# Groups' rows in a ViT block with routed experts: loaded as 32x32 blocks and transposed by VectorE

## What is computed

```python
xt = x.reshape(-1, d)                               # 2304 tokens x 192, after layernorm
route_prob = softmax(xt @ Ws + bs, axis=-1)         # 9 experts
p, routes = max(route_prob), argmax(route_prob)
h = gelu(einsum('td,edf->tef', xt, W1) + b1)        # 192 -> 768
out = einsum('tef,efd->ted', h, W2) + b2            # 768 -> 192
common = out[:, 0, :]
sel = out at routes
final = where(routes == 0, common * scaling, pe * sel + (1 - pe) * common)
```

## Time and profile before

| | us |
|---|---|
| median of 3 runs | 387.95 |
| lowest and highest | 387.5, 389.18 |
| the profiled execution | 386.88 |
| its span, first to last instruction | 385.0 |
| TensorE clock granted, mean over the span | 0.993 |

### The profile page before, as it was taken

The page is one execution under the profiler, slowest core; times in us unless marked ns, Lnnn a source line. Parts: engine busy times, 40 slices in busy tenths (PEclk is TensorE's granted clock), DMA queues, the critical chain, the costliest instruction groups (busy, mean ns, idle before and its releaser), DMA issues. The chain is left out here.

```text
span 385.0 us, 10445 instructions
## 1 busy us (share of the span) xinstructions
PE 364.3 (95%) x3291; PEld 325.6 (85%) x3292; DVE 172.2 (45%) x595; ACT 163.9 (43%) x553; POOL 188.3 (49%) x307
## 2 busy tenths in 40 slices
PE   6799999999999999899999999998999999999991
PEld 5677877788888888788888899997999999999991
DVE  3365767777777787544232265411112211111111
ACT  0122233333333354778444454335545544555540
POOL 1657977777777787443013006740333333444333
PEclk9999999999999999999999999999999999999997
DMA  7764335353321435435000905626666776676630
GB/s 243 234 207 120 101 105 162 94 156 91 90 79 48 130 113 166 124 97 187 20 0 14 245 2 142 217 80 147 150 170 160 176 187 164 167 165 164 155 76 0
DMA packets 40589, 49.58 MB, mean 129 GB/s; under 512 B 10412, under 2 KB 32313, under 8 KB 40553
## 3 DMA queue, kind: packets, MB, share of 16 engines
q1 hardware_dynamic: 34641, 42.95, 37.8%
q0 software_dynamic: 5024, 5.72, 8.8%
q10 hardware_dynamic: 888, 0.45, 0.4%
HBM read 39.84 MB, written 10.27 MB: 130 GB/s over the span
## 5 line engine op out<-in xcount | busy, mean ns | idle before, releaser
L641 PE MATMUL bank<-W,ARENA 128*128 (+1 forms) x516 | 94.6, 334 | 1.5 <-issue 1.2
L641 PEld LDWEIGHTS bank<-W,ARENA 128*128 128x128 f32 x516 | 82.8, 190 | 5.7 <-issue 1.5
L1371 POOL DMA_INDIRECT out<-ARENA,ID x25 | 39.4, 1575 | 71.3 <-DVE ARENA L1236 62.0
L855 ACT ACTIVATE ARENA<-score_banks,B1R 128x128 f32<-128x128 f32 x150 | 41.5, 376 | 39.8 <-PE score_banks L631 24.1
L855 ACT ACTIVATE ARENA<-score_banks,B1T 128x128 f32<-128x128 f32 x108 | 29.9, 375 | 31.8 <-PE score_banks L631 31.8
L1269 POOL TENSOR_TENSOR VS<-V,R 108x384 f32<-108x384 f32 x32 | 27.7, 865 | 30.5 <-DVE R L960 30.2
L1232 DVE TENSOR_TENSOR ARENA<-bank,B 128x192 f32<-128x192 f32 x25 | 8.9, 358 | 71.6 <-PE bank L641 71.6
L623 PE MATMUL score_banks<-RINGS,W1R 128*128 128x128 f32 x300 | 37.8, 276 | 1.4 <-ACT RINGS L795 0.8
L623 PEld LDWEIGHTS score_banks<-RINGS,W1R 128*128 128x128 f32 x300 | 35.6, 192 | 1.8 <-issue 1.8
L1260 POOL TENSOR_TENSOR RINGS<-QK,GM 128x216 f32<-128x216 f32 x64 | 34.1, 553 | 3.4 <-PE score_banks L579 3.4
L579 PEld LDWEIGHTS score_banks<-QK,RINGS 48*108 48x108 f32 x512 | 28.7, 171 | 6.1 <-issue 2.9
(11 more groups left out here) (149 smaller groups left out, 622.1 us busy)
## 6 DMA issues: line engine op xcount, KB each, us to landing
W1R<-in_w SPq DMA_DIRECT2D x25, 384.0 KB
V<-v_rows SPq DMA_DIRECT2D x96, 54.0 KB
W<-in_w SPq DMA_DIRECT2D x9, 576.0 KB, 4.2
W1R<-in_w_rest SPq DMA_DIRECT2D x50, 96.0 KB
ARENA<-in_patches SPq DMA_DIRECT2D x11, 384.0 KB, 3.6
packed_tokens<-RINGS POOLq DMA_DIRECT2D x1, 2425.0 KB, 13.2
ARENA<-packed_tokens SPq DMA_DIRECT2D x25, 97.0 KB, 2.8
PT<-in_patches SPq DMA_DIRECT2D x6, 384.0 KB, 3.2
```

Of the source, the lines that this page charges most:

```text
L641: last = pe.matmul(bank[2 * par][:, 0:D], HT[par][:, c * P:c * P + P], W2[:, bass.ds((expert * FC + c) * D, D)], start=c == 0, stop=c == F ...
L855: last = act.activation(HT[par][:, to:to + P], bank[6 + g][:, c * P:c * P + P], ACT.Gelu, bias=b1[:, bias:bias + 1])
L1371: pool.indirect_dma_start(out, bass.IndirectOffsetOnAxis(ap=ID[par][:, 0:1], axis=0), YR[par], None, bounds_check=TOKENS - 1, oob_is_err=F ...
```

## The change

`load_blocks` takes the place of the load of a group's rows. A row of 192 features is 6 blocks of 32. For each block f one DMA moves all 128 rows' 32 numbers: with row = 32 j + b, it puts row b's of the four j side by side on partition b (plus 32 times f % 4), 32x4x32 numbers in pieces of 128 bytes. So each 32x32 square in `XF[par]` is one square of the rows, at the place where its transpose belongs. The share and the number that stand behind the 192 features in a row are not loaded into XF any more; they came from SLOT_ROWS already. DVE transposes the squares of XF[par] into XTF[par] in one instruction for features 0 to 127 and two for the other 64, once for each half of the partitions. PE's transposes, ACT's copies and the semaphore `ffn_t_done` go; SP now waits for `ffn_xt` before it loads into XF[par] again.

```diff
--- before.py
+++ after.py
@@ -48,6 +48,7 @@
 WCOLS = DFF + FH
 EXPERTS = 9
 EPS = 1e-5
+BLOCK = 32
 
 
 GROUPS = (TOKENS + (EXPERTS - 1) * (P - 1)) // P
@@ -153,7 +154,7 @@
         VST = [cut(D) for _ in range(2)]
         marks[0] = 0
         HT = [cut(DFF) for _ in range(2)]
-        XF = [cut(ROW) for _ in range(2)]
+        XF = [cut(2 * P) for _ in range(2)]
         YR = [cut(D) for _ in range(2)]
         BASE = [cut(D) for _ in range(4)]
         RT = cut(8 * TE)
@@ -281,7 +282,6 @@
         h2_aggr = sem("h2_aggr")
         h2_rstd = sem("h2_rstd")
         xn2_ready = sem("xn2_ready")
-        ffn_t_done = sem("ffn_t_done")
         ffn_xt = sem("ffn_xt")
 
         f1_done = sem("f1_done")
@@ -395,6 +395,14 @@
                 expert = sp.value_load(GROUP_EXPERT[0:1, bass.ds(n, 1)], min_val=0, max_val=EXPERTS - 1)
                 load_up(W1R[par], expert, w1_in[par])
 
+            def load_blocks(n, par):
+
+                rows = packed[bass.ds(n * P, P)] if not isinstance(n, int) else packed[n * P:n * P + P]
+                for f in range(D // BLOCK):
+                    row, at = f % (P // BLOCK) * BLOCK, f // (P // BLOCK) * P
+                    sp.dma_start(XF[par][row:row + BLOCK, at:at + P].rearrange("b (j a) -> b j a", a=BLOCK),
+                                 rows[:, f * BLOCK:(f + 1) * BLOCK].rearrange("(j b) a -> b j a", b=BLOCK)).then_inc(xr_in[par], 16)
+
             def load_down(e, landed):
                 cols = bass.ds(e * FC * D, FC * D)
                 sp.dma_start(W2[:, cols], w2[:, cols]).then_inc(landed, 16)
@@ -463,7 +471,7 @@
 
             sp.wait_ge(scattered, 16 * TILES)
             for r in range(2):
-                sp.dma_start(XF[r], packed[r * P:r * P + P]).then_inc(xr_in[r], 16)
+                load_blocks(r, r)
             sp.dma_start(SLOT_ROWS[:, :].rearrange("p (g w) -> p g w", w=2),
                          packed.rearrange("(g p) w -> p g w", p=P)[:, :, D:ROW]).then_inc(slot_rows_in, 16)
             for t in range(BASES_FIRST, BASES_SECOND):
@@ -471,8 +479,8 @@
 
             def load_group(i, ks):
                 n, par, half = tile_at(i, ks[0])
-                sp.wait_ge(ffn_t_done, n - 1)
-                sp.dma_start(XF[par], packed[bass.ds(n * P, P)]).then_inc(xr_in[par], 16)
+                sp.wait_ge(ffn_xt, n - 1)
+                load_blocks(n, par)
                 if ks[0] == 2:
                     for t in range(BASES_SECOND, TILES):
                         store_base(t)
@@ -666,13 +674,6 @@
                 pe.matmul(bank[0][:, 0:EXPERTS], x[:, 0:P], WR[:, 0:EXPERTS], start=True, stop=False)
                 pe.matmul(bank[0][:, 0:EXPERTS], x[0:DB, P:2 * P], WR[0:DB, EXPERTS:2 * EXPERTS],
                           start=False, stop=True).then_inc(router_done, 1)
-
-            def transpose_group(i, k):
-                n, par, half = tile_at(i, k)
-                pe.wait_ge(xr_in[par], 16 * (half + 1))
-                if k >= 2:
-                    pe.wait_ge(ffn_xt, n - 1)
-                transpose_tile(XF[par], bank[4 + par]).then_inc(ffn_t_done, 1)
 
             def transpose_xn2(t):
                 pe.wait_ge(xn2_ready, t + 1)
@@ -750,13 +751,8 @@
                                   MIXER_START, MIXER_START + 1, MIXER_START + 2, UP_START, UP_START + 1),
                       (TILES,) * 4 + (PAIR_STEPS,) * 2 + (TILES,) * 5)
 
-            for n in range(2):
-                transpose_group(0, n)
-
             def group_step(i, ks):
-                kt, kf, kh = ks
-                if kt is not None and kt >= 2:
-                    transpose_group(i, kt)
+                kf, kh = ks
                 if kf is not None:
                     n, par, half = tile_at(i, kf)
                     pe.wait_ge(w1_in[par], 48 * (half + 1))
@@ -771,7 +767,7 @@
 
             pe.wait_ge(groups_ready, 1)
             pe.wait_ge(expert_w_in, 16 * EXPERTS)
-            two_by_two(pe, group_step, (0, 1, 2), GROUPS)
+            two_by_two(pe, group_step, (1, 2), GROUPS, start=1)
 
 
         @block.scalar
@@ -888,24 +884,13 @@
             each_step(main_step, (1, 2, 4, SCORE_LAG, WEIGH_LAG, MIXER_START, MIXER_START + 1, UP_START),
                       (TILES,) * 3 + (PAIR_STEPS,) * 2 + (TILES,) * 3)
 
-            def copy_group(n, par):
-                act.wait_ge(ffn_t_done, n + 1)
-                copy_twice(XTF[par], bank[4 + par]).then_inc(ffn_xt, 1)
-
             def group_step(i, ks):
-                kx, kg = ks
-                if kx is not None and kx >= 2:
-                    n, par, half = tile_at(i, kx)
-                    act.wait_ge(f1_done, 2 * (TILES + n - 1))
-                    copy_group(n, par)
-                if kg is not None:
-                    n, par, half = tile_at(i, kg)
-                    act.wait_ge(b1_copied, n + 1)
-                    gelu(TILES + n, par, B1R[par], True)
-
-            for n in range(2):
-                copy_group(n, n)
-            two_by_two(act, group_step, (0, 1), GROUPS)
+                kg, = ks
+                n, par, half = tile_at(i, kg)
+                act.wait_ge(b1_copied, n + 1)
+                gelu(TILES + n, par, B1R[par], True)
+
+            two_by_two(act, group_step, (0,), GROUPS)
 
 
         @block.vector
@@ -1075,6 +1060,9 @@
                 if s == MIXER_START + TILES + 2:
                     slots()
                     scatter_shares()
+                if s == MAIN_END - 1:
+                    for n in range(2):
+                        transpose_group(n, n, 0, False)
                 if ky is not None:
                     add_common(ky)
                 if s == MIXER_START + TILES + 2:
@@ -1187,6 +1175,16 @@
                     dve.wait_ge(gelu_done, 2 * (TILES + n - 1))
                 dve.tensor_copy(B1R[par][:, :], B1T[:, bass.ds(expert * FC, FC)]).then_inc(b1_copied, 1)
 
+            def transpose_group(n, par, half, guard):
+
+                dve.wait_ge(xr_in[par], 16 * (D // BLOCK) * (half + 1))
+                if guard:
+                    dve.wait_ge(f1_done, 2 * (TILES + n - 1))
+                dve.transpose(XTF[par][:, 0:P], XF[par][:, 0:P])
+                for g in range(2):
+                    last = dve.transpose(XTF[par][g * DB:g * DB + DB, P:2 * P], XF[par][0:DB, P:2 * P])
+                last.then_inc(ffn_xt, 1)
+
             def base(t):
 
                 if t >= 4:
@@ -1222,6 +1220,7 @@
                 kw, kh = ks
                 if kw is not None:
                     n, par, half = tile_at(i, kw)
+                    transpose_group(n, par, half, True)
                     copy_b1(n, par, True)
                 if kh is not None:
                     n, par, half = tile_at(i, kh)
```

## The result

The changed kernel takes **427.7 us** in the median (426.05 to 435.68), the kernel before on the same chip 389.2 us. The ratio is **1.102, interval 1.0988 to 1.1052**: slower by a tenth, near the forecast of 432 us and inside its range. Now and then an execution of any of these kernels shows a lower granted clock in the stages ahead of the groups and takes some 10 us more: it counts in the medians and not in the ratios, and where a profile is of such a one (the first of the changed kernel, "long pieces", "four of six by ScalarE") only its groups are read.

What follows compares the result with a forecast made beforehand. PE bounds the groups now; SP's issue would after the change: group 24 at 276.6 + 22 x 6.30 = 415.2, 44.5 us later, 386.88 + 44.5 = 431.4, so 432 us in the median, range 408 to 455.

Steps and rivals of the forecast that it cites:

- The bound now, and SP's spare time: Groups of routed tokens: PE bounds at 4.57 us a group; SP needs 3.2 us, leaving 1.4 us.
- Part 1: PE in the groups: loses two transposes, 0.22 us a group while PE bounds; ScalarE's three lost copies gain nothing.
- Part 2: VectorE in the groups: three transposes, 1.1 us at 0.36 each, 3.2 us at three times that; no cost taken.
- part 5: Start of the groups: 12 issues, 5.6 us; groups 0 and 1 1 to 2 us late; group 2 starts at 276.6.
- Part 3: SP in the groups: five more DMAs, issue 0.42 us each, need 6.30 us a group (5.52 to 7.38), setting the period.
- rival B: SP's queue in the groups: one issue stall of 0.9 us per group, 20 us more, 452 us; chance 7%.
- rival A: Groups: SP stays hidden, PE stays the bound, 5.3 us less, some 1.4 more at the start, 384 us; chance 5%.
- Part 4: DMA engines in the groups: 768 pieces of 128 bytes instead of 128 of 776, hidden, no cost taken.
- The sum: Whole kernel: group 24 starts 44.5 us later, 431.4 us profiled, 432 us median; cheap end 412, dear end 460.
- C: PE in the groups: idling drops the clock to 1.2 GHz, up to 8.7 us a group, 485 us; chance 4%.
- D: SP's issues cheaper than any row, SP and PE nearly meet: within 0.5%, chance 2%; slower by up to 5%, 2%.

Runs made afterwards that it cites:

- long pieces: Changed kernel with each of its six loads per group bringing 32 rows of 128 contiguous numbers, 192 pieces where there are 768: 433.42 us, ratio 1.102.
- four of six by ScalarE: Changed kernel with four of the six block loads per group issued from ScalarE's queue, two from SP's: 391.78 us, ratio 1.008.
- the stores first: Changed kernel with the stores of tiles 12 to 15 issued before the loads of groups 0 and 1: 423.66 us, ratio 1.094.

## Why the prediction was right, and where two of its terms were not

**The bound now, and SP's spare time: right.** 1.4 us left per group for five more issues was the number on which it turned. SP, which waited for PE 15 times before, waits for nobody in the groups now. Five more issues on the kernel before cost what the whole change costs, and one load instead of six leaves PE without a gap.

**Part 1, PE's transposes: right.** 4.57 to 4.35 us is seen where SP isn't the bound.

**Part 2, VectorE at no cost: right in the loop.** Groups of DVE's lines, columns as on the page:

```profile
L1183 DVE STREAM_TRANSPOSE RINGS<-ARENA 128x128 f32<-128x128 f32 x25 | 7.8, 311 | 44.5 <-DMA ARENA<-packed_tokens 38.6 <-PE score_banks L639 5.9
```

```profile
L1185 DVE STREAM_TRANSPOSE RINGS<-ARENA 64x128 f32<-64x128 f32 x50 | 14.1, 283 | 0.3
```

Three take 0.31 + 2 x 0.283 = 0.88 us a group, less than even the cheap price of 0.36 each (1.1 us). At the start it was wrong, see part 5.

**Part 3, SP's need: right in kind, 5% too dear in size.** The stage ran at (407.98 - 276.17) / 22 = **5.99 us** a group, forecast 6.30 with bounds of 5.52 and 7.38. The mis-sized term is the issue of a 32x4x32 block:

```profile
L403 SPq DMA_DIRECT2D ARENA<-packed_tokens x150: 316/317/441, 260.0 to 406.6; - x150
```

It takes 0.317 us, not 0.42. I had taken the nearest rows by source and breadth; the lowest of the rows, the 0.29 us of L411 (36 partitions with two runs each, though 0.374 in its median), was nearer. Six issues with the five addresses between them took 2.83 to 2.92 us instead of 3.47: 0.6 us a group, 13 us over 22 groups. The other terms were each a little short (forecast in brackets): L389 to the end of L391 1.62 us (1.59), the pause behind them 0.20 and 0.70 in turn, 0.45 in the mean (0.38), the expert's number and addresses with the address behind the loads 0.92 and 1.02 (0.86). With a few stalled issues (below, rival B) they take 0.3 us a group, 6 us over 22 groups, back. That leaves 6.8 us less than forecast.

The Trainium skill's sentence that starting a DMA is "usually small relative to the DMA itself" ("DMA: Bandwidth & Descriptors", section Issuing engines are not separate DMA queues), taken as a rule for the sum, would have given rival A's 384 us. For one DMA the trace agrees: the issue of L389 takes 0.36 us and the landing 3.4. But transfers overlap and the issues of one queue don't: the DMA engines were 57% busy while that queue set the time. So the sum of the issues can't be left out here, small as each one is. What the same section says of starting DMAs from several engines, that it saves the time of the sequencer, is what the kernel with four loads on ScalarE shows: there it is worth 36 us (427.6 to 391.8).

**Part 4, small packets: right.** A quarter of the block pieces gave the same period.

**Part 5, the start: one step failed.** "Groups 0 and 1 start 1 to 2 us late and this is inside that time" left out who waits on DVE. I moved 12 issues ahead of SP's stores and costed them for SP's own queue, but did not ask who waits for these stores. `base(16)` does, and the change had put the transposes of groups 0 and 1 behind it. Before, this wait was short and hurt nobody, since PE transposed the rows itself. DVE's line in the kernel before:

```profile
262.45 0.42 DVE L1194 SCALAR_TENSOR_TENSOR ARENA<-QK,KEEP,H 128x192 f32<-128x192 f32 x1 [1.49 <-DMA out<-ARENA]
```

Now it is 6.87 us, and the first up product starts 10.9 us behind the first load where it started 4.2 behind it (261.94 - 257.73): 6.7 us later, not 1 to 2. "Inside that time" failed too. From the first block load to L389 of group 2 it was to take 13.87 us (257.73 to 271.6) and took 16.17 (260.00 to 276.17), 2.3 us more, and these are SP's two waits shown above: 1.2 us in front of the blocks of group 2, until DVE had transposed group 0 and XF was free, and 1.1 us in front of L395, until PE had done the up product of group 0, at half the clock, and W1R was free. With the stores first both are gone, and it took 11.8. One step came out by two errors that met: twelve issues took 5.56 us as forecast (5.6), but with 0.317 us each and 0.16 between them instead of 0.42 and 0.045.

**The sum, term by term**, forecast 431.4 us for the profiled execution. The stage ahead of the groups ended 2.27 us later than in the profile of before (260.00 against 257.73; in the run with the stores first it was 258.01), ahead of all that the change touches: +2.3. The start: +2.3. From L389 to the up product of group 24 (407.98 to 412.39) 4.4 instead of 5.0: -0.6. 22 periods: -6.8. The tail behind it 14.5 instead of 14.3: +0.2. That is 428.8, and 428.73 was measured. So errors of both signs met: with the forecast's period the time would have been 435.6, 4.2 us above the forecast; without SP's two waits at the start 426.5, 4.9 us below it. And the period itself met by two errors: over the 22 groups the issues were priced 13 us too high and the rest 6 us too low. The closeness of 427.7 to 432 is partly luck; the range is not.

**The rivals.** A (SP hidden): the six issues would have had to fit into 1.74 us to cost nothing, and four take 1.82. B (stalls): they don't repeat. A few pairs of L391 took 1.27 to 1.98 us instead of 1.16; without them the mean period would be 5.92, so they cost 1.6 us in all. C (the clock halves in the groups): not between 300 and 400 us, with gaps of 0.8 to 2.0 us in front of L631. Once in the groups it did, behind a longer gap:

```profile
293.54 2.92 PE L631 MATMUL score_banks<-RINGS,W1R 128*128 128x128 f32 x12 [2.17 <-DMA W1R<-in_w_rest]
```

The window of these products has a granted clock of 0.50. It cost nothing further on: L389 of this group and the next stand 5.77 us apart all the same (294.81 and 300.58), and SP had no wait for PE. At the start it did cost, behind the gap of 8.4 us, which my forecast didn't contain. D came nowhere near.

## What to carry to other kernels

Count the DMAs that one queue must issue per pass, each with its address and the value loads behind it, and hold the sum against the pass's time on the bound engine: here nine issues needed 5.99 us where 4.35 were there, and the bytes played no part. When work moves into another engine's queue, ask of each wait in front of its new place who will now stand behind it. An engine that the change has relieved is the first place to look for the issues: ScalarE took four of six, and with the stores ahead of the first loads a loss of 10% became a gain of 0.7%.

## What the runs showed of the hardware beyond that

- The issue of a DMA of 32 partitions with four runs of 128 bytes takes SP 0.317 us, one of 32 rows of 512 bytes 0.334 in the median. Twelve with fixed addresses took 5.56 us, 0.48 us from start to start; with the address from a register it is 0.50 to 0.52. From ScalarE's queue the first kind takes 0.333 us.
- VectorE's transpose of 32x32 blocks in fp32 takes 0.311 us for 128x128 and 0.283 us for 64x128: half the rows save a tenth of the time.
- With PE idle for 22% of the time, in gaps of 0.8 to 2.0 us in front of L631, the granted clock stayed at 1.00 (2.4 GHz) from 300 to 400 us. Behind gaps of 8.4 and of 2.17 us it stood at 0.50 (1.2 GHz) and twelve products took 2.90 and 2.92 us instead of 1.50. With the stores first it fell behind a gap of 2.07 us, and the second group's twelve products, behind one of 1.11, took 2.90 us too; with four loads on ScalarE and the stores first, gaps of 1.65 and 1.11 us at the same place left it at 1.00 (1.58 and 1.62 us). What decides between these cases stays open.
- Whether fewer, larger loads of the up-weights (the two of L391 take 1.16 us of each period) would give the change its room on SP alone was not tried.
